# A product of 512 columns that nobody reads, placed before each wait for shifted queries, in a four-layer decoder kernel

## What is computed

```
x = _layernorm(x + _L0_attn_ref(x, ...))           # stage rec
x = _layernorm(x + _L0_xattn_ref(ctx_1024, x, ...)) # stage x0, 16 heads of 8 channels
x = _layernorm(x + _L0_ffn_ref(x, ...))             # stage f0, 8 experts
...                                                 # a1, x1, f1, a2, x2, f2, a3, x3
x = _layernorm(x + _L3_ffn_ref(x, ...))             # stages f3 and ex: attention and 8 experts
```

## Time and profile before

| what | us |
|---|---|
| median of 3 runs | 5395.16 (5385.72 to 5404.15) |
| profiled execution | 5404.53 |
| its span, first to last instruction | 5402.4 |
| TensorE busy with products | 4678.8 |
| VectorE busy | 3461.3 |
| ScalarE busy | 2388.2 |
| GpSimd busy | 641.3 |

### The profile page before, as it was taken

How to read it: one execution, slowest core, us unless ns; L and a number is a source line. 1 busy time by engine, 2 the same in 40 slices (tenths; PEclk the granted TensorE clock), 3 DMA queues, 4 the chain that set the end, 5 groups by cost and what they waited for, 6 DMA issues and landing times.

```text
span 5402.4 us, 131265 instructions
## 1 busy us (share of the span) xinstructions
PE 4678.8 (87%) x55657; PEld 3405.6 (63%) x55657; DVE 3461.3 (64%) x9345; ACT 2388.2 (44%) x4855; POOL 641.3 (12%) x713
## 2 busy tenths in 40 slices
PE   5667888899898989998989989889998989988787
PEld 4345666567666666776666666666676766666555
DVE  7754666755666676667676566767756676655654
ACT  3323444444535444444554444454445455443432
POOL 5550000010001001100010110000101010010000
PEclk7668899899999999999999999999999999999999
DMA  1131110012010001211100111010120101001001
GB/s 62 28 98 32 32 33 2 9 34 73 16 56 18 19 19 32 65 39 36 33 2 27 41 48 50 24 33 13 30 62 20 50 16 33 27 27 40 9 23 38
DMA packets 160340, 181.80 MB, mean 34 GB/s; under 512 B 62890, under 2 KB 90642, under 8 KB 158994
## 3 DMA queue, kind: packets, MB, share of 16 engines
q1 hardware_dynamic: 159762, 173.42, 10.8%
HBM read 162.52 MB, written 10.55 MB: 32 GB/s over the span
## 4 chain that ended last, share of the span: by engine, by line
PE 62%; DVE 15%; ACT 8%; issue 5%; DMA 1%; POOL 1%; SPq 1%; POOLq 0%; DVEq 0%; ACTq 0%
PE g_bank L2750 8%; PE g_bank L2765 8%; PE g_bank L1645 6%; PE g_bank L1617 5%; ACT g_keys_exps L1698 5%; PE g_bank L1668 5%; DVE g_tops L1720 4%; PE g_bank L2013 2%; PE g_bank L2003 2%; PE g_bank L1630 2%; PE g_bank L1451 1%; PE g_bank L1679 1%; PE g_bank L2096 1%; PE g_bank L2351 1%; PE g_bank L2332 1%
## 5 line engine op out<-in xcount | busy, mean ns | idle before, releaser
L1698 ACT ACTIVATE g_keys_exps<-g_bank 128x512 f32<-128x512 f32 (+1 forms) x1536 | 798.1, 596 | 606.0 <-PE g_bank L1645 605.2
L1720 DVE TENSOR_REDUCE g_tops<-g_bank 128x4 f32<-128x512 f32 (+1 forms) x1536 | 809.0, 575 | 347.9 <-PE g_bank L1617 345.2
L1430 POOL TENSOR_TENSOR g_rstd<-g_rstd,minus_half 128x4 f32<-128x4 f32 x224 | 226.5, 1011 | 4242.1 <-DVE g_rstd L1412 4235.6
L2765 PEld LDWEIGHTS g_bank<-region,g_keys_exps 128*128 128x128 f32 x4096 | 516.7, 192 | 153.8 <-issue 140.3
L2750 PE MATMUL g_bank<-g_xT,region 128*128 128x512 f32 x1024 | 551.8, 620 | 9.8 <-ACT g_keys_exps L2778 4.0
L2765 PE MATMUL g_bank<-region,g_keys_exps 128*128 128x128 f32 x4096 | 548.0, 278 | 6.3 <-DVE g_base L2797 5.5
L1645 PE MATMUL g_bank<-g_qa,g_keys_exps 32*77 32x128 f32 (+1 forms) x12288 | 458.7, 286 | 65.8 <-DVE g_o L1741 32.6
L1645 PEld LDWEIGHTS g_bank<-g_qa,g_keys_exps 32*77 32x77 f32 (+1 forms) x12288 | 381.8, 170 | 171.4 <-DVE g_o L1741 63.7
L1617 PE MATMUL g_bank<-g_keys_exps,g_qa 32*128 32x154 f32 (+1 forms) x6144 | 392.0, 366 | 96.8 <-ACT g_keys_exps L1698 81.5
L1668 PE MATMUL g_bank<-g_keys_exps,g_v 77*32 77x128 f32 (+1 forms) x12288 | 432.7, 284 | 46.5 <-DVE g_tops L1720 33.3
L1668 PEld LDWEIGHTS g_bank<-g_keys_exps,g_v 77*32 77x32 f32 (+1 forms) x12288 | 326.3, 113 | 158.2 <-DVE g_tops L1720 92.2
(11 more groups left out here) (377 smaller groups left out, 8405.0 us busy)
## 6 DMA issues: line engine op xcount, KB each, us to landing
region<-L_w_in SPq DMA_DIRECT2D x512, 256.0 KB, 2.9
region<-xT_in SPq DMA_DIRECT2D x16, 256.0 KB, 2.7
z_scratch<-m_z SPq DMA_DIRECT2D x4, 1024.0 KB, 5.0
g_oT_sc<-z_scratch SPq DMA_DIRECT2D x64, 64.0 KB, 2.4
g_xT<-xT_in SPq DMA_DIRECT2D x16, 256.0 KB, 3.2
g_o<-x_in SPq DMA_DIRECT2D x16, 256.0 KB, 3.4
out<-g_x SPq DMA_DIRECT2D x16, 256.0 KB, 2.3
setup_weights<-prepared_in SPq DMA_DIRECT2D x1, 2589.5 KB, 11.2
```

Of the source, the lines that this page charges most:

```text
L1430: e.tensor_tensor(g.rstd[:, :], g.rstd[:, :], g.s["minus_half"], ALU.pow).then_inc(*b.gpsimd(st + " rstd"))
L1698: e.activation(g.p[0:nk, r, :, :], bank[r][0:nk, :].rearrange("p (u q) -> p u q", u=4), ACT.Exp, scale=scale).then_inc(*b.scalar(f"{st} p ...
L1720: e.tensor_reduce(top_columns(g, r), src, AX, ALU.max).then_inc(*b.vector(f"{st} top {n} {r}"))
L2765: ins = e.matmul(bank[1][:, n * D:(n + 1) * D], g.gated_hid[:, x % 2, c, n * T:(n + 1) * T], weights.part(f"w2 {x}", c), start=c == n == 0 ...
```

## The change

One line is added in attention_tensor, between the yield after the transposes of the maxima and the wait for the shifted queries. It multiplies one identity by all four (128 rows by 128 columns of weights, 512 columns moving, bf16) into bank[3]. No semaphore is raised by it and nothing reads its result; the products of the same step then overwrite bank[3] (with masked keys those of line 1640, else those of line 1645). The wait, and all other instructions, stay as they are. The step runs four times in each of six stages in each of 16 batches, 384 times in all.

```diff
--- before.py
+++ after.py
@@ -1630,6 +1630,7 @@
             ins = e.transpose(bank[2][:, t * T:(t + 1) * T], top_rows(g, t), g.k["ident"])
         ins.then_inc(*b.tensor(f"{st} tops turned {n}"))
         yield
+        e.matmul(bank[3][:, :], g.s["ident4"][:, 0, :], g.s["ident4"][:, :, :], start=True, stop=True)
         e.wait_ge(*b.vector[f"{st} q shifted {n}"])
         if n:
             e.wait_ge(*b.scalar[f"{st} oT {n - 1}"])
```

## The result

The changed kernel takes 5468.2 us (median of 4 runs, 5462.8 to 5479.2), the kernel before on the same chips 5399.7 us. The ratio is 1.0127, with a 95% interval of 1.0108 to 1.0145: 1.3% slower, +68.6 us (+58 to +78) where +49 us was forecast. The profiled execution has a span of 5470.2 us, 67.8 us more than that of before.

The account below looks back on a forecast made before the run. After the opening the kernel was taken as bound by TensorE, with waits on VectorE and ScalarE between. Path 56, low clock level +1 and returned clock -8 gave +49 us: 5395 to 5444 us, range +25 to +75 us (chance 0.70).

Parts of the forecast that it names:

- How often the place waits: Before lines 1645 and 1640: TensorE idle 113 of 384 times, 76.8 us; products there free, 28 us if uncovered.
- Price behind wide work: Where work over all 128 rows stands before the step: the new product costs its columns, 0.226 us.
- Price behind narrow work: Where narrow products stand before the step: columns plus one change of shape, 0.226 + 0.086 = 0.31 us.
- The share on the path: At the 271 places without idle: 0.82 of 68 us of new TensorE work reaches the end, 56 us.
- The clock: After the opening: filling 28 of 569 us of idle returns 5% of 162 us lost, 8 us.
- A sign that could not fail: Prediction wrong if TensorE's idle time in 1200 to 4800 us (337 us) falls as much as busy time grows.
- TensorE's busy time: Over the profile after the change: up by some 70 to 90 us, with products near 0.38 us mean duration.
- The third rival: At the 271 places: every product 0.31 us, all on the path, nothing from the clock; 84 us, 5479 us; chance 0.10.
- The first rival: After the opening: filled lulls return most of 162 us; with two thirds, -51 us, 5344 us; chance 0.08.

Follow-up runs that it names:

- cols64: Against the kernel before: the added product at all 384 places, with 64 columns instead of 512; ratio 1.0054, +29 us.
- lulls_early2: Against the kernel before: 28 products of 256 columns in 7 lulls, two of 512 in each of 76 waits for shifted queries; ratio 0.9951, -26 us.

## Why the prediction was right, and where it was off

The direction and the mechanism held: the time lies inside the range, and at 308 of 384 places no own transposes stand in front. The number stands near the upper end of "+25 to +75 us", and its interval reaches beyond it. Step by step:

- **How often the place waits: right.** 113 cases with 76.8 us of idle were counted. The idle time fell by 29 us (28 forecast), the covered product costs next to nothing, and taking the cover away costs 36 us (28 forecast: the change of shape was left out of that figure).
- **Price behind wide work: right.** 0.226 us from the difference of two rows; 0.20 us on average and 0.22 us in the example.
- **Price behind narrow work: too small.** 0.31 us was taken; it is 0.37 us on average and 0.43 us in the example. The step added columns and one change of shape. But there are two changes, into the wide product as well as out of it, and the distances of cols64 show them almost bare: 0.24 us in the example. As only a third of the places without a wait are narrow ones, the price over all of them was still met: 84 x 0.37 + 184 x 0.20 = 68 us of work by the trace, and 271 x 0.25 = 68 us in the prediction.
- **The share on the path: probably too low.** 0.82 was taken. The part of the loss that isn't the clock's, 63 us, is 0.93 of the 68 us. It was 0.97 for the narrow places alone (30 of 84 x 0.37 = 31 us) and 0.92 for the wide ones (34 of 184 x 0.20 = 37 us). Forecast for that part were 56 us of path and 1 us for the low level. The 6 us missing are this share; with intervals of 10 us to either side, 0.82 itself isn't excluded.
- **The clock: nothing was given back.** -8 us was taken by a proportion, as if each filled microsecond of idle time brought back its share of the lost clock. The loss went from 303 to 312 us, some +6 us of time, give or take 5. That is 14 of the 20 us by which the sum was short. One product of 0.22 us a place buys no clock, covered or not (301 against 300 us); it takes more at one spot. The loss even rises in some of the kernels whose products stand mostly in the path (322, 321, 321 and 316 us), and in others it hardly does (307 and 303 us with the narrow or the wide places alone). Up to 6 us of a rise only say that the same clock stands over a longer time; what makes the rest isn't settled. The rise of the change itself is within its error.
- **A sign that could not fail.** The prediction was to be wrong if TensorE's idle time in 1200 to 4800 us fell by as much as its busy time grew. It did, from 337 to 304 us, while the busy time grew by 33 us, but in a stretch of fixed length the two always add up to its length. Over the whole span the busy time grew by 108 us, the idle time fell by 41 us, and the span grew by the difference, 68 us.
- **TensorE's busy time** was to rise by 70 to 90 us and rose by 108 us. The product is shown with its modelled 0.38 us, of which the engine's neighbours overlap less than I assumed; the time wasn't computed from this.

The third rival, every product at 0.31 us, all of it on the path and nothing from the clock, gave +84 us. That is 15 us above the measured time, where the forecast is 20 us below it, and two of its three terms came out closer to the runs: nearly all is on the path, and the clock gives nothing. The share and the clock were both off to the same side, and the range was just wide enough for it; that part is luck.

The first rival, the clock that pays, was rightly held unlikely for this change. What it says is true of other places and doses: lulls_early2 gains by it. The argument against it, that the lull in front of a fall is another wait and not the edited one, fits the later runs: the wait for the exponentials shown above is such a lull. The Trainium skill, "TensorE: Matmul & The Clock Gate", "A second HAM failure mode: psum-queue depth-cycling", has one kernel in which frequent short idles between groups of products send the clock back and forth. With the covered waits filled once the loss stayed at 301 us, so this case doesn't bear it out at that dose; with them filled twice it fell from 303 to 289 us, which agrees with it.

## What to carry to other kernels

Before putting warming work in front of a wait, count how often the engine is really idle there. In a fixed interleaved order most waits are over when the engine reaches them, and there the work is plain cost on the path of the bounding engine. If the clock is to be kept, fill the few long lulls, behind which the clock falls, and the waits that directly follow the same program's step, with more than one product each, and judge it by the mean clock of many runs: one pair of traces showed a gain in a lull where there was none. A product over all rows between groups over 32 rows costs up to twice its columns; over 32 rows alone it can run beside them.

## What the runs showed of the hardware

- A product over 128 rows between two groups over 32 rows, lines 1617 and 1645, adds 0.24 us with 64 columns and 0.43 us with 512. With 512 columns over 32 rows it doesn't delay the start of the second group (0.63 us with and without it) and adds 0.10 us in all. Behind a product over 128 rows 512 columns add 0.22 us.
- With four or six products of 256 columns in a wait of 2.7 us the granted clock stayed at 1.00 in three of three traces; without them it fell to 0.50 there in eleven of eleven. Behind another lull, of 2.6 us, it fell with and without them.
- The kernel before loses some 300 us of full-clock work in a run, and 23 of its runs differ in time by 0.62 us for each microsecond by which they differ in that loss (0.37 to 0.72 in the other sets of its runs).
- 28 products of 256 columns in 7 lulls, beside one of 512 in each of 76 waits, lower the loss by 21 us; the 76 alone don't lower it.
